# Making the last late keys and values, and loading the first expert rows, at the end of the first stage

## The reference

```python
x = x + L0_xattn(layernorm(x), ctx, ctx, Wq, bq, Wk, bk, Wv, bv, Wo, bo)   # 8 heads over the sequence axis
x = x + L0_ffn(layernorm(x), W_gate, b_gate, W_e, b_e)
x = x + L1_xattn(layernorm(x), ctx, ctx, Wq, Wk, Wv, Wo)                   # 8 key/value heads, groups of 4
x = x + L1_ffn(layernorm(x), w_gate, b_gate, w_up, b_up, w_down, b_down)   # silu(gate) * up, inner size 1376

def L0_ffn(x, W_gate, b_gate, W_e, b_e):          # 8 experts, the best 2 of each row
    _, top_idx = top_k(x @ W_gate + b_gate, 2)
    y_all = relu(einsum('bsd,edh->bseh', x, W_e) + b_e)
    return take_along_axis(y_all, top_idx[..., None], axis=2).mean(axis=2)
```

## Time and profile before

| what | us |
|---|---|
| runs of the kernel before | 884.24, 885.11, 882.51 (median 884.24) |
| the profiled execution | 884.15 |
| its span in the profile | 882.4 |
| TensorE busy in the span | 845.8 (96%) |
| VectorE, ScalarE, GpSimd busy | 433.5, 346.2, 284.0 |
| mean granted TensorE clock | 0.989 of full speed |

### The profile page before, as it was taken

How to read it: one execution, slowest core, us unless ns; L and a number is a source line. 1 busy time by engine, 2 the same in 40 slices (tenths; PEclk the granted TensorE clock), 3 DMA queues, 4 the chain that set the end, 5 groups by cost and what they waited for, 6 DMA issues and landing times.

```text
span 882.4 us, 19749 instructions
## 1 busy us (share of the span) xinstructions
PE 845.8 (96%) x7585; PEld 689.5 (78%) x7585; DVE 433.5 (49%) x839; ACT 346.2 (39%) x567; POOL 284.0 (32%) x401
## 2 busy tenths in 40 slices
PE   5999997899999989999999999999999999999996
PEld 4888877788888867777777788878887888878885
DVE  4999974244444688888888722133221312222112
ACT  3666653233333466666666622222221122211110
POOL 3578884000000778877753321130020002002000
PEclk9999998799999999999999999999999999999999
DMA  8477678595553634554422431010120003010001
GB/s 277 144 252 252 232 251 274 198 333 187 164 163 113 209 111 136 164 147 134 125 58 58 139 118 60 24 33 1 46 87 12 1 13 108 0 63 34 1 0 49
DMA packets 55389, 105.29 MB, mean 119 GB/s; under 512 B 8226, under 2 KB 12322, under 8 KB 55042
## 3 DMA queue, kind: packets, MB, share of 16 engines
q1 hardware_dynamic: 48530, 85.02, 30.2%
q0 software_dynamic: 5120, 16.78, 5.9%
q10 hardware_dynamic: 1648, 2.23, 0.7%
HBM read 68.02 MB, written 35.98 MB: 118 GB/s over the span
## 4 chain that ended last, share of the span: by engine, by line
PE 74%; issue 2%; POOL 2%; ACT 2%; DVE 1%; DMA 0%; SPq 0%; DVEq 0%; ACTq 0%; POOLq 0%
PE c_ps L1277 9%; PE c_ps L1279 9%; PE c_ps L1278 9%; PE c_bank L1801 4%; PE c_bank L1315 3%; PE c_bank L1316 3%; PE c_bank L1321 3%; PE c_bank L1807 3%; PE c_bank L1802 3%; PE c_bank L1865 3%; PE c_ps L1840 2%; PE c_bank L1014 2%; PE c_bank L1015 2%; PE c_bank L1020 2%; PE c_po L1015 2%
## 5 line engine op out<-in xcount | busy, mean ns | idle before, releaser
L1354 DVE SCALAR_TENSOR_TENSOR d_hid<-c_ps,d_b_up,d_silu 128x512 f32<-128x512 f32 (+1 forms) x44 | 33.0, 751 | 227.4 <-PE c_ps L1279 227.4
L1277 PE MATMUL c_ps<-d_nT_hi,gate_up_hi 128*128 128x512 f32 (+1 forms) x352 | 139.9, 398 | 0.0
L1279 PE MATMUL c_ps<-d_nT_hi,gate_up_lo 128*128 128x512 f32 (+1 forms) x352 | 138.6, 394 | 0.0
L1278 PE MATMUL c_ps<-d_nT_lo,gate_up_hi 128*128 128x512 f32 (+1 forms) x352 | 138.3, 393 | 0.0
L1233 ACT ACTIVATE d_silu<-c_ps,d_b_gate 128x512 f32<-128x512 f32 (+1 forms) x44 | 30.3, 689 | 141.6 <-PE c_ps L1279 141.6
L1193 POOL TENSOR_TENSOR late_x<-late_x,d_b_down 128x512 f32<-128x512 f32 x16 | 21.5, 1377 | 187.9 <-DMA late_x<-x_after_attention 187.9
L1279 PEld LDWEIGHTS c_ps<-d_nT_hi,gate_up_lo 128*128 128x128 f32 (+1 forms) x352 | 65.2, 185 | 16.6
L1278 PEld LDWEIGHTS c_ps<-d_nT_lo,gate_up_hi 128*128 128x128 f32 (+1 forms) x352 | 65.4, 186 | 15.8
L1277 PEld LDWEIGHTS c_ps<-d_nT_hi,gate_up_hi 128*128 128x128 f32 (+1 forms) x352 | 65.3, 185 | 15.4
L1240 ACT ACTIVATE d_hid_hi<-d_hid 128x512 fp32r<-128x512 f32 (+1 forms) x44 | 27.8, 632 | 125.7 <-DVE d_hid L1354 125.7
L1044 ACT ACTIVATE b_rowsT_hi<-c_bank 128x512 fp32r<-128x512 f32 x39 | 23.4, 599 | 82.0 <-PE c_bank L1003 82.0
(11 more groups left out here) (308 smaller groups left out, 1930.9 us busy)
## 6 DMA issues: line engine op xcount, KB each, us to landing
b_rows<-expert_rows SPq DMA_DIRECT2D x39, 256.0 KB, 2.9
expert_results<-b_result SPq DMA_DIRECT2D x39, 256.0 KB, 2.5
a_wstage<-L_ffn_W_e SPq DMA_DIRECT2D x16, 512.0 KB, 4.2
late_x<-x_after_attention SPq DMA_DIRECT2D x28, 256.0 KB, 3.7
c_stage<-gate_up SPq DMA_DIRECT2D x16, 344.0 KB
out<-late_x SPq DMA_DIRECT2D x16, 256.0 KB, 2.8
x_after_attention<-late_x SPq DMA_DIRECT2D x12, 256.0 KB, 3.7
c_y_in<-x_after_attention SPq DMA_DIRECT2D x12, 256.0 KB, 2.8
```

The lines of the kernel that those rows point to most:

```text
L1277: pe.matmul(bank[0:w, :], gu_hi[:, cols], nT_hi[:, g % 2, k, :], start=k == 0, stop=False)
L1278: pe.matmul(bank[0:w, :], gu_hi[:, cols], nT_lo[:, g % 2, k, :], start=False, stop=False)
L1279: mm = pe.matmul(bank[0:w, :], gu_lo[:, cols], nT_hi[:, g % 2, k, :], start=False, stop=k == KD - 1)
```

## The change

1. Item 4 is made by TensorE at step m = 18, ahead of the rank of the last tile. Behind the count come items 5, 6 and 7; `keep_kv` and `store_kv` go to item 7, and the making, copying and storing of item 7 leave the second block.
2. SyncE, at the end of the first block, waits until the table is there (24 counted steps of VectorE), reads the places of blocks 0 to 3, waits for all scatters, and issues the four loads of rows; then it issues the first half of the bias. The second block loads rows from block 4 on. The rows' buffers and semaphores are now made outside both blocks. They lie where they lay, over buffers that the first block uses, so waits for those buffers' last readers stand ahead.
3. GpSimd's scatters of tiles 12 to 15 are issued without waiting for the scatters of two tiles earlier.

```diff
+            def load_bias(half):
                 sp.wait_ge(o_made, TILES)
+                if half:
+                    sp.wait_ge(w_lo, TILES)
+                else:
+                    sp.wait_ge(y_made, TILES)
+                    sp.wait_ge(l_made, TILES)
...
+            def load_first_rows():
+                sp.wait_ge(table_step, TABLE_STEPS)
+                first = [sp.value_load(shared["table"][0:1, 0, b:b + 1], min_val=0, max_val=EXPERTS * REGION - P) for b in range(ROWS_RING)]
                 sp.wait_ge(w_lo, TILES)
+                sp.wait_ge(xt_made, TILES)
+                for i in range(2):
+                    sp.wait_ge(scattered[i], 16 * TILES)
+                for b in range(ROWS_RING):
+                    sp.dma_start(shared["rows"][:, b, :], shared["xs"][bass.ds(first[b], P), :]).then_inc(shared["rows_loaded"][b], 16)
...
-            for i in range(2, KV_LATE - 1):
+            for i in range(2, KV_LATE):
...
             for i in range(2):
                 sp.wait_ge(x1_stored[i], 8 * TILES)
-                sp.wait_ge(scattered[i], 16 * TILES)
+            load_first_rows()
+            load_bias(0)
...
-                want(pool, scattered[t % 2], 32 * (t // 2))
+                if t < 2 * KEPT:
+                    want(pool, scattered[t % 2], 32 * (t // 2))
...
-            for i in range(4, KV_LATE - 1):
+            for i in range(4, KV_LATE):
                 keep_kv(i)
...
+                if m == TILES + 2:
+                    make_late_k(4)
+                    make_late_v(4)
                 if tile(m - 3) and m >= TILES:
                     make_rank(m - 3)
...
-            for i in range(4, KV_LATE - 1):
+            for i in range(5, KV_LATE):
                 make_late_k(i)
                 make_late_v(i)
...
         for b in range(BLOCKS + 6):
-            if b < BLOCKS:
+            if RING <= b < BLOCKS:
                 load(b)
-            if b == 1:
-                cols = slice(0, EXPERTS * DIM // 2)
-                sp.dma_start(bias[:, cols], b_e.rearrange("e h -> (e h)")[cols].partition_broadcast(P)).then_inc(shared["bias_loaded"][0], 16)
-            if b == 3:
-                sp.wait_ge(kv_kept, 1)
-                sp.dma_start(shared["kv"][last, :, :], kv_stage[:, 0:KV_COLS]).then_inc(last_stored, 16)
...
     def tensor(pe):
-        for k in range(KD):
-            pe.matmul(kv_bank[:, 0:P], wk1[:, k, :], ctx_rows[:, k, :], start=k == 0, stop=k == KD - 1)
-        for k in range(KD):
-            mm = pe.matmul(kv_bank[:, P:2 * P], ctx_rows[:, k, :], wv1[:, k, :], start=k == 0, stop=k == KD - 1)
-        mm.then_inc(kv_made, 1)
         pe.wait_ge(const_made, 1)
```

More of the change, by code:

```diff
@@ L115 @@
 KV_EARLY, KV_LATE, KV_COLS, X_RING = 8, 8, P + 16 * (HD + 1), 6
+ROWS_RING, TABLE_STEPS = 4, 24
 SBUF_END = 229344
@@ L252, in first_attention @@
         shared["bias"] = nc.alloc_sbuf_tensor_at("expert_bias", [P, EXPERTS * DIM], F32, offset=shared["bias_at"])
-        shared["last_kv"] = wk1, wv1, ctx_in[KV_LATE % 3].rearrange("p (k n) -> p k n", k=KD), kv_stage[(KV_LATE - 1) % 3]
+        shared["rows"] = nc.alloc_sbuf_tensor_at("expert_rows_in", [P, ROWS_RING, DIM], F32, offset=shared["bias_at"] + 4 * EXPERTS * DIM)
         moved = lo_end[:, 5 * DIM:5 * DIM + 16 * TILES].rearrange("p (t e) -> p t e", e=8)
@@ L374, in _ @@
                 if i == 2:
-                    load_bias()
+                    load_bias(1)
                 store_kv(i)
@@ L937, in experts @@
     biased, result = sb("biased", [P, 2, DIM]), sb("result", [P, 3, DIM])
[L938 to L941, removed]
+    bias, rows, rows_loaded = shared["bias"], shared["rows"], shared["rows_loaded"]
     pt, py = banks[0:2], banks[2:4]
-    rows_loaded, stored = [sem(f"ex_rows_loaded{i}") for i in range(RING)], [sem(f"ex_stored{i}") for i in range(3)]
+    stored = [sem(f"ex_stored{i}") for i in range(3)]
     t_made, hi_kept, lo_kept, y_made = sem("ex_t_made"), sem("ex_hi_kept"), sem("ex_lo_kept"), sem("ex_y_made")
     biased_made, result_made = sem("ex_biased_made"), sem("ex_result_made")
-    kv_made, kv_step, kv_kept = sem("ex_kv_made"), sem("ex_kv_step"), sem("ex_kv_kept")
-    wk1, wv1, ctx_rows, kv_stage = shared["last_kv"]
-    last, last_stored = KV_LATE - 1, shared["kv_stored"][(KV_LATE - 1) % 3]
     table, halves = shared["table"], ((shared["gu_hi"], shared["gu_lo"]), shared["ex23"])
@@ L1029, in scalar @@
     def scalar(act, in_front_of_last):
-        def keep_last_kv():
-            act.wait_ge(kv_made, 1)
-            act.wait_ge(last_stored, 16 * (last // 3))
-            act.activation(kv_stage[:, 0:P], kv_bank[:, 0:P], ACT.Copy).then_inc(kv_step, 1)
-            values = kv_stage[:, P:KV_COLS].rearrange("p (b j r d) -> p b j r d", b=2, j=4, r=2)
-            for r in range(2):
-                for c2 in range(2):
-                    made = kv_bank[64 * c2:64 * c2 + 64, P:2 * P].rearrange("p (j r d) -> p j r d", j=4, r=2)
-                    ins = act.activation(values[64 * r:64 * r + 64, c2, :, r, 0:HD], made[:, :, r, :], ACT.Copy)
-                    ins.then_inc(kv_kept if r and c2 else kv_step, 1)
         def keep_high(b):
@@ L1054, in scalar @@
         for b in range(BLOCKS + 2):
-            if b == 0:
-                keep_last_kv()
             if b < BLOCKS:
@@ L2121, in ffn_phase @@
         shared["kv_stored"] = [kept.sem(f"kv_stored{i}") for i in range(3)]
+        shared["rows_loaded"] = [kept.sem(f"rows_loaded{i}") for i in range(ROWS_RING)]
         shared["bias_loaded"] = [kept.sem(f"bias_loaded{i}") for i in range(2)]
```

10 lines of the change are left out of this document (5 added, 5 removed).

## The result

The changed kernel took 886.58 us in the median of 12 runs (885.17 to 889.66), the kernel before 883.3 in 12 runs of the same chip (881.83 to 885.84): a ratio of 1.0037, with a 95% interval from 1.0025 to 1.0049. That is 3.3 us more where 0.8 less was predicted. The ratio of e9 leaves out one execution of 1491.63 us, in a slow state with a granted clock of 0.768.

A forecast was written before the change was run, and what follows sets the result against it. TensorE, busy nearly everywhere, was taken as the bound, so only its idle time counts. First product's start -0.5 and clock -0.4 make -0.9 us on 884.15, written as 883.4 us; range 881.2 to 886.0.

The forecast's parts named there:

- K: End of ScalarE's copy of item 7, ahead of the barrier: put at 151.5, own range 150.8 to 152.4.
- upper bound: Latest end of item 7's copy, with items 6 and 7 at the low clock level from 146.4: 155.0.
- rival 2: Earlier scatters take DMA engines from contexts, TensorE stands ahead of items 6 and 7, clock falls: 886.8 us, chance 0.14.
- F: Start of the first product on TensorE behind the barrier: put at 160.9 against 161.37 before, -0.5 us.
- break-even: End of item 7's copy from which the first product's delay exceeds what the clock gives back: 152.9.
- F = K + 9.36: From item 7's copy to first product: store, row loads, bias half, waits, barrier, identity, two transposes, 9.36 us.
- Six DMAs in one row: SyncE's DMAs ahead of the barrier were to stand in one row, 5.2 us long.
- the scatters' early end: Late scatters issued without waits, done by 150: gain nothing, as SyncE waited for item 6, not for them.
- The clock: First product: 4.1 us at the low level in place of 5.0, -0.4 us; no low stretch on items 5 to 7.
- The sum: Whole kernel: -0.5 for the first product's start and -0.4 for the clock, -0.9 us on 884.15.

The follow-up runs named there:

- e9: Changed kernel with SyncE's table reads and row loads ahead of item 6's store and the scatters' waits put back; ratio 0.9979 to the kernel before.
- e1: Changed kernel with the scatters' waits put back; ratio 1.0020 to the kernel before.
- e5: Changed kernel with the second bias half issued behind the store of item 5; ratio 1.0016 to the kernel before.
- e11: Changed kernel unaltered, run again for a second profile; ratio 1.0035 to the kernel before.
- h13: Changed kernel with the second bias half issued behind the store of item 5, run again for a second profile; ratio 1.0003 to the kernel before.
- h14: Changed kernel with four more unused table reads in SyncE's list ahead of the row loads; ratio 1.0055 to the kernel before.
- e4: Changed kernel with table reads and four row loads issued ahead of the store of item 6; ratio 0.9979 to the kernel before.
- e10: Kernel before with item 3 made behind the count; ratio 0.9998 to the kernel before.
- e3: Changed kernel with row loads and first bias half back in the second block, SyncE's scatter wait ahead of the barrier; ratio 1.0029 to the kernel before.

## Why the prediction was wrong, step by step

**The step that failed is the term K**, the end of ScalarE's copy of item 7: put at 151.5, measured at 155.37, above my upper bound of 155.0. In it the transfers were mis-sized. The context of item 6 I let land 5.0 us after its issue (141.26 to 146.3); it took 8.0. That of item 7, also 5.0, took 8.8. No row of the kernel before shows the landing of that transfer, only that it was in use 8.15 us after its issue (141.26 to 149.41). My bounds, 2.66 and 6.9 us from the nearest rows, did not hold it either: the row of 6.9 us was for the bias half, and I read it as the most that a transfer could take there, though a small one behind it on full engines took longer than the large one (8.0 and 8.8 us against 6.6 for the bias half in the changed kernel). With 407 GB/s in the hole, the engines delivered about the 415 of the earlier trace rows; that the contexts stood behind the rest is my reading of it. The 3.9 us of K are 2.4 us of later start of item 6 (148.76 against 146.4) and 1.6 us of low clock on items 6 and 7, which I had at the high one (they took 5.5 us for 3.9), less 0.1 of rounding and hand-over.

**A second term of K was put at nothing without a reason: the stores.** ScalarE can copy item i only when the store of item i-3 has landed, and the sum has no such wait. In the changed kernel the copy of item 5 stood 3.5 us for the store of item 2. The stores of items 3 and 4 landed at 150.3 and 151.8. Had the contexts come as I said, and the stores as they did, the copy of item 7 could have started only at 151.8 and ended at about 152.9, an estimate from these landings: 1.4 us over my K by itself. Here the late context hid it.

**That is rival 2 in its mechanism, and by luck nearly to the number**: K 155.0, F 164.4, 886.8 us against 155.37, 165.05 and 886.58. Its K was items 6 and 7 all at the low clock from 146.4 on; measured are a later start and less of the low clock. Its 886.8 had -0.4 for the clock and nothing given back, and so stands beside a median, not beside the profile's 885.17. Its break-even was also wrong: by its own terms F is later by more than the clock gives back from K = 152.4 on, not 152.9. I gave it 0.14, since "item 5 fills most of the time before". Item 5 ended at 145.16, 3.6 us ahead of the context. Its mechanism is right (TensorE stands ahead of items 6 and 7, the clock falls), its culprit only in part. e9 has the scatters' waits and the bias half early, and no late signal either; its transfers:

```profile
gu_lo_end<-ctxT SPq DMA_DIRECT2D x1, 256.0 KB, 7.8
a_ctx_own<-ctxT SPq DMA_DIRECT2D x1, 256.0 KB, 7.2
```

In the two profiles of the changed kernel they are 8.0 and 8.8, and 8.0 and 8.7. So early scatters cost item 6's context 0.2 us and item 7's 1.5 to 1.6, by one profile of e9; TensorE still waits 3.40 us for item 6 in e9. What the Trainium skill says (DMA: Bandwidth & Descriptors, "Issuing engines are not separate DMA queues"), that transfers of different issuing engines interleave on the same 16 engines, agrees with the trace: from 140 to 148 us the scatters' queue has 40.7% of the 16 engines' time, beside SyncE's contexts and stores, and the DMA share in the hole is 1.04. I applied it to the scatters and not to the bias half, which lies ahead in the same queue.

**F = K + 9.36 held**: 9.68 in the changed kernel, 9.67 to 9.68 in e1, e5 and e11, 9.93 in h13. Some of that is luck, since two terms missed in opposite directions. Within it, four reads and four issues were put at 4.40 us; from the store's end (155.72) to the bias half (160.97) are 5.25, which holds the reads and issues and 0.85 of waits where I took 0.2. From the end of that issue (161.34) to the opening of the barrier (162.28) are 0.94 us where I took 1.32. The identity behind the barrier stands bare, as said, 0.82 us (162.28 to 163.10) where I took 0.71, and the eight transposes 1.89 for 1.94.

**Six DMAs in one row, no wait for rows, none for the bias**: right, though the row was 5.9 us long (155.40 to 161.34) and not 5.2. So was that the scatters' early end buys nothing.

**The clock**: predicted that 4.1 us of the product run low; measured 1.76 in the first profile, a gain of 1.6 us and not 0.4, and 4.10 in e11, as predicted. Full clock was back 3.65 us behind the first transpose in the one and 6.0 us in the other. The rule of the Trainium skill that I quoted then (TensorE: Matmul & The Clock Gate, "Part 1: The HAM clock gate (the "warmup" mystery)"), that the same kernel can show a different number of slow matmuls, agrees with these two executions. The fall on items 6 and 7 was the part that I said would not come.

**The sum**: by the first profile F +3.7, clock -1.6, some 1.0 given back at the stages' seam: +1.0 on 884.15. By e11 F +4.1, clock -0.4, 1.0 given back at the same place: +2.6 us of span. The ratio over 12 runs is +3.3 us. So the first profile shows little of the loss mainly because its low clock on the product was short. Among the twelve runs the clock has a part too: the mean granted clock goes from 0.982 to 0.991, and the two slowest (889.66 and 889.58 us) have the lowest, 0.982 and 0.983.

## What to carry to other kernels

A load that is moved forward beside a full queue is better priced by the bytes ahead of it than by the time that its neighbour took: 256 KB took 8.0 and 8.8 us here, and at most 3.1 us in h13, where the megabyte came behind it (and the signal was late). An engine that only issues DMAs is a path like any other once a barrier follows: a read with its issue took SyncE about 1.1 us, four more reads came out one for one (h14), and the gain over the changed kernel lay in moving that list into its idle time (e4, 0.9979), not in making it earlier as a whole. What a buffer's last store holds up belongs into the sum, even where another wait hides it. Where two moves are made together, look for what each covered for the other: item 7 hid behind the rows' landing, and the landing behind item 7.

## What was not expected of the hardware

**A matmul's end can be signalled late.** VectorE's first instruction on the last logits started 1.5 to 4.3 us behind the end that the matmul's row shows in 12 of 16 profiles, and 0.04 us behind it in the other four (changed, e9, e10, e11). Of the kernel before:

```profile
138.42 1.06 PE L634 MATMUL a_pr<-a_wg,a_xT 128*128 128x8 f32 x8
...
141.13 0.17 DVE L792 MAX8 a_top<-a_pr 128x8 f32<-128x8 f32 x1 [3.38 <-remote]
```

The matmuls end at 139.48, VectorE starts at 141.13. Neither the scatters' waits nor the bias half decides it (e1, e5 and h13 have it, e9 not), nor item 3 alone (e10 and e11 are both without it). The order of the instructions alone does not decide it either: up to K, the changed kernel, e11, e3 and h14 are the same, and it is on time in the first two and late in the others. What sorts the experiments is the chip: the three profiles from one (e9, e10, e11) are on time, the eleven from the two others late. Whether that is the chip or something else that these runs shared is not shown. It matters to how the profiles are compared: with the late signal TensorE stands at the ranks and items 5 to 7 come later, so that less or nothing is left to wait for at their contexts; without it TensorE waits there. K comes out alike: 155.37 and 155.81 in the two profiles of the changed kernel, 155.44 in h14 and 154.20 in e3, which are the same up to K with the late signal. What causes it stays open.

**A longer hole was not followed by a longer low stretch.** Before, 1.57 us of idle TensorE were followed by 6.83 us at the low level; after, 3.60 us of it by 3.41. In e9, 3.40 us of idle TensorE ahead of item 6 were followed by none: items 6 and 7 ran at a granted clock of 1.00 to their end (152.00 to 155.82).
